# Aggregating a relational graph network with the gathered rows as matmul weights

## The chip, the cores and the metric

The kernel runs on one core of one Trainium2 chip. Its engines are TensorE (PE, with the weight loads shown apart as PEld), VectorE (DVE), ScalarE (ACT), GpSimd (POOL) and SyncE (SP), which share SBUF and run apart, held together by semaphores. The metric is the device time of one launch in microseconds, the median of several runs.

## The reference, cut to what matters

The program is two graph layers, then an attention with random features, then a second attention with low-rank experts. Only the graph layers are touched. There are N = 1250 nodes of D = 768 features, R = 8 relations and 41250 edges, sorted by their destination. One layer is

```
seg  = dst * 8 + etype
sums = segment_sum(x[src], seg);  cnt = segment_sum(1, seg)
mean = (sums / max(cnt, 1)).reshape(N, 8, 768)
out  = einsum('nri,rio->no', mean, W) + x @ root + b
```

Layer 1 is followed by a ReLU, layer 2 takes the result as its x, with its own weights. The 33 edges that a node has on average end in one sum, so that the work can be done as: multiply every node by each of the 8 relation matrices (the messages), fetch for every edge the message of its source and relation, weigh it with 1/cnt, and add it to the row of its destination.

## The kernel before, in words

**Messages.** For each layer and each of 8 relations, PE multiplies 10 blocks of 125 nodes (`RT` = 10, `ROWS` = 125) by a 768x768 panel, in split fp16 (three products of high and low parts, 36 matmuls of 384 columns to a block, `row_products`). ACT and DVE split each result into a high and a low fp16 part (`message_high`, `message`), and SP stores them in DRAM in `msg_table`, one row of 3072 bytes for each node and relation. DVE and ACT meanwhile prepare the next panel (`next_panel`: maximum at t = 0, scales at t = 4, split at t = 6). In layer 1 DVE also counts edges; in the third panel (p = 2, after t = 8) it finds for each group of edges the first and the last block of 125 nodes (`block_extents`), and PE waits for that (`bounds_made`) before the fourth panel.

**Aggregation.** The edges lie in 324 tiles of 128 (`TILES`). POOL fetches each tile with one indirect DMA (L629) into one of `GSLOTS` = 18 slots: 6 in `GATA`, 4 in `ROW`, 2 in `MSG`, and 6 in `WST`, the buffer of the weight panels, so that these last 6 wait for the panel's split (`w_lo`). Tiles are taken in groups of `AT` = 3, 108 groups in 18 turns of 6. For each group PE and DVE loop over the blocks of 125 nodes that it touches; one such step is a pass. There are 117 passes in a layer. In a pass DVE makes for each tile a matrix `HOT` of 128 edges by 125 nodes, which holds the edge's weight where its destination is the node, in a high and a low part (L1280). PE takes `HOT` as weights and moves the gathered rows (L1747): 3 products x 2 halves x 3 tiles = 18 matmuls of 384 columns. The sums lie in PSUM with a node in each partition; DVE adds them to `ROOT`, 125x768 (L1262, `take_pass`), three passes late (`LAG_PASS` = 3). A small matmul of zeros ahead of each group (L1736) tells POOL by the semaphore `group_read` that earlier slots may be filled again: POOL's group g waits for the start of group g - 5.

**The root panel.** x @ root takes 10 more blocks of 36 matmuls. The first 5 run before the passes, the others between turns (`ROOT_AT`). DVE adds each to `ROOT` (L1239), which ACT had set to the bias.

**Between the layers.** DVE takes the maximum of `ROOT` (L1169), from which a scale is made. For each of the 10 blocks ACT writes the ReLU into `ROW`, PE transposes it (6 transposes, L1558) into two PSUM banks, and ACT and DVE split it into the high and low parts of `HT`, feature by node (L732, L1187). The products of the block follow. DVE's order is: `h_low(t)`, the message of block t - 1, `next_panel` for t - 1.

**After layer 2.** The semaphore `rows_done` tells PE to begin the next stage (L1780) and SP to load its next weights and to store `ROOT` in DRAM (`gnn_rows`). Then SP loads `WPR` and three vectors.

The call of the pass loop, where PE waits:

```
pe.wait_ge(S["pass_out"], n + (LAG_PASS * L + 2))
for k in range(AT):
    pe.wait_ge(S["hot_made"], n * AT + (k + 1))
    pe.wait_ge(S[f"gat_in{slot}"], i * 16 + (16 * TURNS * L + 16))
    for hp, mp in ((0, 0), (0, 1), (1, 0)):
        for h in range(2):
```

## Time and profile before

| what | value |
|---|---|
| median of 3 runs | 3300.21 us (3297.36 to 3302.02) |
| span of the profiled execution | 3506.0 us; no other time of this execution is shown |
| mean granted TensorE clock | 0.960 of full speed |
| PE busy | 3182.0 us, 91% |
| DVE busy | 1850.6 us, 53% |
| POOL busy | 1290.4 us, 37% |
| ACT busy | 783.8 us, 22% |
| chain that ended last, by line | L1612 (products of blocks) 25%, L1747 (passes) 20%, L1963 5% |

The span reaches from the first to the last instruction of one execution under the profiler. It is 205.8 us longer than the median of the runs. "Idle before, releaser" says what ended the idle time of an engine: "issue" is that nothing which the profile shows was waited for, and "remote" that the releaser is another core or a queue it does not know. Stages of the span: products of layer 1 to about 597 us, aggregation of layer 1 to 1141 us, products of layer 2 to about 1650 us, aggregation of layer 2 to 2191 us, the two attentions to 3506 us.

### The profile page before, as it was taken

What the parts mean: (1) busy time and instruction counts of PE and PEld (TensorE: products, weight loads), DVE (VectorE), ACT (ScalarE), POOL (GpSimd) and SP (SyncE); (2) the same over time, 40 slices, a digit from 0 to 9 for tenths busy, and PEclk for the clock granted to TensorE, in tenths of its full rate; (3) what the DMA queues carried; (4) which work ended last, traced back from release to release, by engine and by line L of the source; (5) the groups of instructions that cost most, each with busy time, mean ns of one, the idle gap of its engine ahead of it and who ended that gap; (6) DMA issues with size and microseconds to landing.
All of it is one profiled execution on the core that took longest, in us unless ns stands there. A gap on an engine that the chain in (4) does not pass through costs nothing.

```text
span 3506.0 us, 63388 instructions
## 1 busy us (share of the span) xinstructions
PE 3182.0 (91%) x19507; PEld 2353.7 (67%) x19508; DVE 1850.6 (53%) x3025; ACT 783.8 (22%) x1113; POOL 1290.4 (37%) x1388
## 2 busy tenths in 40 slices
PE   6999999888888799999888888999987799999999
PEld 5788888666666688888666666677665555555555
DVE  6576666655555433333555555333458755566551
ACT  1211212000000312122000000444521354544550
POOL 2681112566555000001566655100042156434662
PEclk9999999999999999999999999999999899999999
DMA  4334344677776232324677776300033000000003
GB/s 146 107 121 129 116 143 147 202 246 253 236 241 224 79 110 94 117 93 141 213 247 257 244 242 208 125 13 27 13 89 93 19 19 19 1 19 19 19 25 95
DMA packets 101107, 433.91 MB, mean 124 GB/s; under 512 B 19582, under 2 KB 19920, under 8 KB 96757
## 3 DMA queue, kind: packets, MB, share of 16 engines
q0 software_dynamic: 55712, 266.87, 23.6%
q1 hardware_dynamic: 42533, 124.83, 11.3%
q10 hardware_dynamic: 2736, 40.50, 3.3%
q8 instruction: 83, 1.36, 0.2%
q14 instruction: 43, 0.35, 0.0%
HBM read 355.21 MB, written 76.88 MB: 123 GB/s over the span
## 4 chain that ended last, share of the span: by engine, by line
PE 75%; DVE 11%; issue 8%; DVEq 3%; ACT 2%; POOL 1%; DMA 1%; another core or an unknown queue 0%; POOLq 0%; ACTq 0%; SPq 0%
PE PS L1612 25%; PE PS L1747 20%; PE PS L1963 5%; PE PS L1780 3%; PE PS L1621 3%; PE PS L1893 2%; PE PS L1788 2%; DVE NMC L1534 2%; PE PS L1950 2%; PE PS L1825 2%; PE PS L1809 1%; PE PS L1951 1%; PE PS L1799 1%; PE PS L1817 1%; POOL PL L683 1%
## 5 line engine op out<-in xcount | busy, mean ns | idle before, releaser
L1612 PE MATMUL PS<-WHL,XT 128*125 (+1 forms) x3240 | 557.1, 331 | 15.5 <-issue 6.5
L1612 PE MATMUL PS<-WHL,HT 128*125 (+1 forms) x3240 | 535.5, 327 | 3.7 <-issue 2.5
L1612 PEld LDWEIGHTS PS<-WHL,XT 128*125 128x125 f16 (+1 forms) x3240 | 443.9, 139 | 106.0 <-issue 16.1
L1612 PEld LDWEIGHTS PS<-WHL,HT 128*125 (+1 forms) x3240 | 442.9, 137 | 90.3 <-issue 3.8
L1262 DVE SCALAR_TENSOR_TENSOR ROOT<-PS,GS,ROOT x240 | 244.3, 1018 | 339.7 <-remote 136.9
L683 POOL TENSOR_TENSOR PL<-PF 125x500 bf16<-125x500 f32 (+1 forms) x360 | 322.6, 930 | 216.8 <-ACT PF L897 216.0
L1280 DVE SCALAR_TENSOR_TENSOR HOT<-NODE,DSTF,WHLO (+1 forms) x702 | 298.8, 476 | 129.4 <-issue 120.2
L1123 DVE SCALAR_TENSOR_TENSOR MSG<-PS,MSG 125x768 f16<-125x768 f32 x160 | 153.0, 956 | 361.0 <-ACT MSG L722 359.5
L1747 PE MATMUL PS<-GATA,HOT 128*125 128x384 f16 x1440 | 278.9, 353 | 49.6 <-issue 45.1
L722 ACT ACTIVATE MSG<-PS 125x768 f16<-125x768 f32 x160 | 129.7, 811 | 775.4 <-PE PS L1612 770.3
L1747 PE MATMUL PS<-WST,HOT 128*125 128x384 f16 x1404 | 265.4, 346 | 41.4 <-issue 39.2
L1747 PEld LDWEIGHTS PS<-GATA,HOT 128*125 x1440 | 205.8, 148 | 108.1 <-issue 64.0
L629 POOL DMA_INDIRECT WST<-msg_table,SKEY x216 | 212.3, 983 | 154.5 <-issue 59.3
L629 POOL DMA_INDIRECT GATA<-msg_table,SKEY x216 | 211.4, 979 | 143.7 <-issue 59.7
L1747 PEld LDWEIGHTS PS<-WST,HOT 128*125 x1404 | 197.2, 145 | 96.5 <-issue 56.1
L1963 PE MATMUL PS<-PF,V 125*128 125x500 bf16 (+1 forms) x720 | 244.7, 352 | 16.0 <-POOL PL L683 14.5
L897 ACT ACTIVATE PF<-PS,QK 125x500 f32<-125x500 f32 (+1 forms) x360 | 213.7, 609 | 124.0 <-PE PS L1951 117.8
L1307 DVE RECIPROCAL RCPF<-PS 64x500 f32<-64x500 f32 (+1 forms) x36 | 99.5, 2764 | 198.6 <-PE PS L1963 198.6
L1747 PE MATMUL PS<-ROW,HOT 128*125 128x384 f16 x912 | 174.9, 347 | 23.1 <-issue 21.9
L561 POOL TENSOR_SCALAR LOWHOT<-IOTA,LOF 128x160 bf16<-128x160 bf16 x162 | 151.8, 954 | 96.2 <-DVEq L980 52.0
L1534 DVE TENSOR_REDUCE NMC<-PS 125x2 f32<-125x1000 f32 (+1 forms) x180 | 173.4, 1021 | 18.0 <-PE PS L1931 16.2
L570 POOL TENSOR_SCALAR TMPF<-ETF,GW 128x324 f32<-128x324 f32 x14 | 19.2, 1374 | 420.9 <-DVE GW L1119 417.3
(293 smaller groups left out, 4433.9 us busy)
## 6 DMA issues: line engine op xcount, KB each, us to landing
msg_table<-MSG SPq DMA_DIRECT2D x160, 336.0 KB
WST<-in_wg_dram ACTq DMA_DIRECT2D x16, 2304.0 KB, 10.0
WST<-in_wf_dram SPq DMA_DIRECT2D x7, 1536.0 KB, 6.7
KROW<-key_rows POOLq DMA_DIRECT2D x54, 192.0 KB, 3.8
msg_table<-MSG SPq DMA_DIRECT2D x160, 39.0 KB
WST<-in_wm_dram SPq DMA_DIRECT2D x5, 1152.0 KB, 5.1
GATA<-msg_table,SKEY POOLq DMA_INDIRECT x216
WST<-msg_table,SKEY POOLq DMA_INDIRECT x216
```

The source lines that it names most:

```text
L561: ins = g.tensor_scalar(LOWHOT[:, e % RING, k, :], IOTA[:], LOF[:, e * GRP + k:e * GRP + k + 1], None, ALU.is_equal)
L629: g.indirect_dma_start(out=gat_slot(k), out_offset=None, in_=msg_table, in_offset=bass.IndirectOffsetOnAxis(ap=SKEY[:, t:t + 1], axis=0)). ...
L683: g.tensor_tensor(PL[:, n_ % PARTED, 0:n], PF[:, n_ % PARTED, 0:n], PH[:, n_ % PARTED, 0:n, 1], ALU.subtract).then_inc(S["ffn_lo"], 1)
L722: act.activation(halves(MSG[0:ROWS, t % 2, 0:D]), rowps(2 * (t % 2)), ACT.Copy, scale=MSG_DOWN[L]).then_inc(S["msg_hi"], 1)
L897: act.activation(PF[:, n_ % PARTED, 0:n], p, ACT.Exp, scale=QK[0:ROWS, SSCALE]).then_inc(S["ffn_act"], 1)
L1123: v.scalar_tensor_tensor(halves(MSG[0:ROWS, t % 2, D:2 * D]), rowps(2 * (t % 2)), MSG_DOWN[L], halves(MSG[0:ROWS, t % 2, 0:D]), ALU.mult, ...
L1262: v.scalar_tensor_tensor(rows, pass_psum(n), GS[0:ROWS, 2:3], rows, ALU.mult, ALU.add).then_inc(S["pass_out"], 1)
L1280: v.scalar_tensor_tensor(hot, node, DSTF[:, bass.ds(t, 1)], weight, ALU.is_equal, ALU.mult).then_inc(S["hot_made"], 1)
L1534: v.tensor_reduce(NMC[:, :, s_, c], PS[0:ROWS, ffn.bank(r):ffn.bank(r) + 2, 0:CHUNKS[c][1]], AX.X, ALU.max).then_inc(S["ffn_dve"], 1)
L1612: ins = pe.matmul(PS[0:ROWS, b0 + h, 0:HALF], X[:, xp, k, bass.ts(t, ROWS)], panel_part(slot, wp, k, h), start=k == 0 and xp + wp == 0, st ...
L1747: ins = pe.matmul(PS[0:ROWS, bass.ds((n % LAG_PASS) * 2 + h, 1), 0:HALF].rearrange("p a c -> p (a c)"), HOT[:, bass.ds((n % HOTS) * AT + k ...
L1963: ins = pe.matmul(o, V2[:, vp, t, h, :], parts[pp], start=t == 0 and vp + pp == 0, stop=t == RT - 1 and vp == 1)
```

## The change

The roles in the pass are exchanged. The gathered rows are the weights (128 edges by 128 features), and what moves is the `HOT` of 32 nodes with its high and low part beside each other, 64 columns, and for the low part of the rows the high half alone, 32 columns. The sums lie feature by node: one PSUM bank of [128, 6 x 2 x 32]. Groups have 4 tiles (81 groups), and the nodes of a group are windows of 32 that begin at the group's own first node, so that a group has as many passes as windows of 32 hold its nodes (for 512 sorted edges at 33 to a node, one pass). The groups are written out one after the other, with a loop over the passes in each. The ring has 12 slots, none of them in `WST`. POOL's group g waits for the end of group g - 3, told by a matmul of zeros behind it.

The root panel, the bias and the accumulator `ACC` lie feature by node too: 18 pieces of 128 features by 500 or 250 nodes, 6 before the passes, the others behind every second group. Layer 2's input is split straight from `ACC`, without transposes. Layer 2's result is transposed at the end: 10 blocks of 6 transposes, with a copy by ACT into one of 4 slots of `ROW`, from which SP stores it; PE waits for the last copy (`gnn_made`), and SP issues its loads of `WPR` and of the vectors ahead of these stores. The bounds of the groups are found in another way: a count over 39 thresholds in place of two comparisons.

```diff
-AT = 3
+AT = 4
 AG = TILES // AT
-GSETS = 6
-LAG_PASS = 3
-HOTS = 4
+GSETS = 3
+GSLOTS = GSETS * AT
+WIN = 32
+WINDOWS = -(-N // WIN)
+COLS = N + WIN
+ROOT_FIRST = 6
+PIECES = [(m, c) for c in range(len(CHUNKS)) for m in range(KT)]
+ROOT_BANK = (6, 3)
...
             sp.dma_start(WST[:, 0:WM], a["wm"][128:256, :]).then_inc(S["w_in"], 16)
-            for b in range(RT):
-                move_rows(sp, gnn_rows[b * ROWS:(b + 1) * ROWS, :], ROOT[:, b, :], S["gnn_out"])
-            sp.wait_ge(S["group_used"], 2 * (AG + 1))
             sp.dma_start(WPR[:], a["wmp"]).then_inc(S["wp_in"], 16)
+            sp.wait_ge(S["group_read"], 2 * AG)
             for n_, key in enumerate(("bmp", "gamma", "beta")):
                 sp.dma_start(VEC[:, n_, :], a[key].broadcast_to([ROWS, D])).then_inc(S["vec_in"], 16)
+            for t in range(RT):
+                sp.wait_ge(S["gnn_made"], t + 1)
+                move_rows(sp, gnn_rows[t * ROWS:(t + 1) * ROWS, :], ROW[:, t % 4, :], S[f"gnn_out{t % 4}"])
...
                 for t in range(TILES):
                     grp, k = t // AT, t % GSLOTS
-                    if t == STAGED:
-                        if L == 0:
-                            edge_weights(0)
-                        g.wait_ge(S["w_lo"], (REL + 1) * (L + 1) + 1)
+                    if t == GSLOTS and L == 0:
+                        edge_weights(0)
+                    if t % AT == 0 and L * AG + grp >= GSETS:
+                        g.wait_ge(S["group_read"], L * AG + grp - GSETS + 1)
...
             def h_high(t):
-                act.wait_ge(S["h_t"], t + 1)
-                act.activation(xtview(HT, 0, t), tview(4), ACT.Copy, scale=HSC[:, HSCALE]).then_inc(S["h_hi"], 1)
+
+                act.activation(HT[:, 0, :, t * ROWS:(t + 1) * ROWS], ACC[:, :, t * ROWS:(t + 1) * ROWS], ACT.Relu, scale=HSC[:, HSCALE]).then_inc(S["h_hi"], 1)
...
+            for t in range(RT):
+                act.wait_ge(S["gnn_t"], t + 1)
+                if t >= 4:
+                    act.wait_ge(S[f"gnn_out{t % 4}"], ROW_IN * (t // 4))
+                act.activation(halves(ROW[:, t % 4, :]), rowps(4 + 2 * (t % 2)), ACT.Copy).then_inc(S["gnn_made"], 1)
...
+                v.tensor_scalar(GB[:, 2:3], GB[:, 1:2], 0.0, None, ALU.is_ge)
+                for m in range(1, WINDOWS):
+                    v.drain()
+                    v.scalar_tensor_tensor(GB[:, 2:3], GB[:, 1:2], float(m * WIN), GB[:, 2:3], ALU.is_ge, ALU.add)
...
                 def h_low(t):
 
+                    v.tensor_scalar(HTMP[:], ACC[:, :, t * ROWS:(t + 1) * ROWS], 0.0, HSC[:, HSCALE], ALU.max, ALU.mult)
+                    v.drain()
                     v.wait_ge(S["h_hi"], t + 1)
-                    v.scalar_tensor_tensor(xtview(HT, 1, t), tview(4), HSC[:, HSCALE], xtview(HT, 0, t), ALU.mult, ALU.subtract).then_inc(S["h_free"], 1)
+                    v.tensor_tensor(HT[:, 1, :, t * ROWS:(t + 1) * ROWS], HTMP[:], HT[:, 0, :, t * ROWS:(t + 1) * ROWS], ALU.subtract).then_inc(S["h_free"], 1)
...
+                def make_hots(grp, p):
+
+                    tiles = slice(grp * AT, (grp + 1) * AT)
+                    v.tensor_tensor(SAME[:], NODE[:, bass.ds(p * WIN, WIN)].unsqueeze(1).broadcast_to([128, AT, WIN]),
+                                    DREL[:, tiles].unsqueeze(2).broadcast_to([128, AT, WIN]), ALU.is_equal)
                     v.drain()
+                    v.tensor_tensor(HOT[:, grp % GSETS], SAME[:].unsqueeze(2).broadcast_to([128, AT, 2, WIN]),
+                                    WHLO[:, tiles, :].unsqueeze(3).broadcast_to([128, AT, 2, WIN]), ALU.mult).then_inc(S["hot_made"], 1)
+
+                def take_pass():
...
+                    columns = ACC[:, :, bass.ds(w0, WIN)]
+                    sums = PS[:, bass.ds(bank, 1), 0:KT * 2 * WIN].rearrange("p a (k w c) -> p (a k) w c", w=2, c=WIN)
+                    for w in range(2):
+                        ins = v.scalar_tensor_tensor(columns, sums[:, :, w, :], GS[:, 2:3], columns, ALU.mult, ALU.add)
...
+                for grp in range(AG):
+                    first = v.value_load(LIM[0:1, grp:grp + 1], min_val=0, max_val=N - 1)
+                    n_passes = v.value_load(PASSES[0:1, grp:grp + 1], min_val=1, max_val=WINDOWS)
+                    v.reg_mov(ready, 1)
+                    with v.Fori(0, n_passes) as p:
+                        v.wait_ge(S["pass_done"], v.snap(ready, min_val=1, max_val=1 << 20))
+                        make_hots(grp, p)
+                        take_pass()
...
+                    if grp % 2 == 0 and grp and r < len(PIECES):
+                        take_root(r)
+                        r += 1
...
+                for grp in range(AG):
+                    n_passes = pe.value_load(PASSES[0:1, grp:grp + 1], min_val=1, max_val=WINDOWS)
+                    pe.reg_mov(taken, 1)
+                    with pe.Fori(0, n_passes):
+                        pe.wait_ge(S["pass_out"], pe.snap(taken, min_val=1, max_val=1 << 20))
+                        pe.wait_ge(S["hot_made"], pe.snap(cnt, min_val=0, max_val=1 << 20) + 1)
+                        for k in range(AT):
+                            t = grp * AT + k
+                            pe.wait_ge(S[f"gat_in{t % GSLOTS}"], 16 * (TILES // GSLOTS * L + t // GSLOTS + 1))
+                            rows = gat_slot(t % GSLOTS)
+                            for c in range(KT):
+                                o = PS[:, grp % GSETS, c * 2 * WIN:(c + 1) * 2 * WIN]
+                                pe.matmul(o, rows[:, c * 128:(c + 1) * 128], HOT[:, grp % GSETS, k].rearrange("p w c -> p (w c)"), start=k + c == 0, stop=False)
+                                ins = pe.matmul(o[:, 0:WIN], rows[:, D + c * 128:D + (c + 1) * 128], HOT[:, grp % GSETS, k, 0, :], start=False, stop=k == AT - 1 and c == KT - 1)
+                        ins.then_inc(S["pass_done"], 1)
...
+                    pe.matmul(PS[:, 7, 320:322], ZERO[:, 0:128], ZERO[:, 0:2], start=True, stop=True).then_inc(S["group_read"], 1)
+                    if grp % 2 and r < len(PIECES):
+                        root_piece(r)
+                        r += 1
 
             pe.wait_ge(S["rows_done"], 2)
+            for t in range(RT):
+                if t >= 2:
+                    pe.wait_ge(S["gnn_made"], t - 1)
+                for k in range(KT):
+                    ins = pe.transpose(PS[0:ROWS, 4 + 2 * (t % 2) + k // 3, (k % 3) * 128:(k % 3 + 1) * 128], ACC[:, k, t * ROWS:(t + 1) * ROWS], IDF[:])
+                ins.then_inc(S["gnn_t"], 1)
+            pe.wait_ge(S["gnn_made"], RT)
```

## Rows read from the trace of the kernel before

**Rows 1.** The page: its head, and a group of weight loads (columns: busy us, mean ns of one, idle before).
```profile
span 3506.0 us, 63388 instructions
...
L1612 PEld LDWEIGHTS PS<-WHL,XT 128*125 128x125 f16 (+1 forms) x3240 | 443.9, 139 | 106.0 <-issue 16.1
```

**Rows 2.** Busy time by stage: length, busy of PE, PEld, DVE, ACT, POOL, clock, DMA.
```profile
630.00:1141.00 511.00, 425.80 (x2358) 331.35 (x2358) 274.86 (x475) 0.00 (x0) 308.61 (x312) 0.92 0.74 241
...
1680.00:2191.00 511.00, 430.17 (x2384) 335.91 (x2382) 276.01 (x475) 0.00 (x0) 304.56 (x312) 0.92 0.74 241
```

**Rows 3.** Groups of POOL's instructions, 630 to 1141 us (a fourth, MSG x34, left out).
```profile
L629 POOL DMA_INDIRECT WST<-msg_table,SKEY x108 | 106.6, 987 | 75.5 <-issue 29.8 <-PE PS L1736 21.4 <-remote 17.6
L629 POOL DMA_INDIRECT GATA<-msg_table,SKEY x102 | 100.2, 982 | 70.5 <-PE PS L1736 31.0 <-issue 26.9 <-remote 12.6
L629 POOL DMA_INDIRECT ROW<-msg_table,SKEY x68 | 67.6, 994 | 38.6 <-issue 16.8 <-PE PS L1736 16.7 <-remote 5.1
```

**Rows 4.** Groups of DVE's instructions in the same stretch.
```profile
L1280 DVE SCALAR_TENSOR_TENSOR HOT<-NODE,DSTF,WHLO (+1 forms) x350 | 148.7, 476 | 59.1 <-issue 54.4
L1262 DVE SCALAR_TENSOR_TENSOR ROOT<-PS,GS,ROOT x120 | 122.1, 1018 | 176.2 <-remote 73.2 <-PE PS L1747 68.0 <-issue 35.1
```

**Rows 5.** The timeline of PE: start, us, what.
```profile
722.52 3.09 PE L1747 MATMUL PS<-GATA,HOT 128*125 128x384 f16 x18
...
725.50 3.09 PE L1747 MATMUL PS<-ROW,HOT 128*125 128x384 f16 x18
```

**Rows 6.** The timeline of all engines, with the idle time before each.
```profile
638.93 1.02 POOL L629 DMA_INDIRECT GATA<-msg_table,SKEY  x1 [0.68 <-issue]
...
657.55 1.02 DVE L1262 SCALAR_TENSOR_TENSOR ROOT<-PS,GS,ROOT  x1 [2.48 <-remote]
...
657.62 4.81 PE L1747 MATMUL PS<-GATA,HOT 128*125 128x384 f16 x18 [1.74 <-issue]
658.07 0.96 POOL L629 DMA_INDIRECT WST<-msg_table,SKEY  x1 [2.56 <-remote]
```

**Rows 7.** The timeline of POOL at the end of layer 1.
```profile
1126.41 1.22 POOL L629 DMA_INDIRECT WST<-msg_table,SKEY  x1 [0.31 <-issue]
```

**Rows 8.** Busy time by stretches of 10 us; the last columns are clock, DMA share, GB/s.
```profile
600.00:610.00 10.00, 9.75 (x55) 7.64 (x54) 3.25 (x15) 0.00 (x0) 5.73 (x6) 0.85 0.89 303
...
1130.00:1140.00 10.00, 9.37 (x57) 7.56 (x57) 4.54 (x7) 0.00 (x0) 0.00 (x0) 1.00 0.02 10
```

**Rows 9.** The chain that ended last: start, us, what.
```profile
578.70 5.85 PE PS L1612 x36
...
1217.18 35.10 PE PS L1612 x216
...
2213.96 10.42 PE PS L1788 x180
...
2259.75 19.03 PE PS L1780 x108
```

**Rows 10.** The timeline between the layers.
```profile
1141.48 8.15 DVE L1169 TENSOR_REDUCE HMX<-ROOT 125x1 f32<-125x7680 f32 x1
...
1156.36 7.53 PE L1612 MATMUL PS<-WHL,HT 128*125 128x384 f16 x36
```

**Rows 11.** The timeline of DVE at two places.
```profile
262.00 0.96 DVE L1123 SCALAR_TENSOR_TENSOR MSG<-PS,MSG 125x768 f16<-125x768 f32 x1 [2.06 <-ACT MSG L722]
...
589.25 0.16 DVE L1131 RECIPROCAL GS<-GS 128x1 f32<-128x1 f32 x1
589.49 0.15 DVE L1133 TENSOR_SCALAR GS<-GS 128x1 f32<-128x1 f32 x1
```

**Rows 12.** The timeline at the end of layer 2's passes.
```profile
2189.76 1.02 DVE L1262 SCALAR_TENSOR_TENSOR ROOT<-PS,GS,ROOT  x1 [1.95 <-PE PS L1747]
...
2193.07 20.88 PE L1780 MATMUL PS<-XT,WHM 128*128 128x500 f16 x108 [3.65 <-issue]
```

**Rows 13.** A DMA issue from 2190 to 2260 us: KB, us to landing.
```profile
WPR<-in_wmp_dram SPq DMA_DIRECT2D x1, 2304.0 KB, 10.6
```

More of the change, by code:

```diff
@@ L61 @@
 PARTED = 6
-ROW_SUMS = (REL + 1) * RT
+ROW_SUMS = REL * RT
 SHIFT = 2.0 ** 15
@@ L1243, in root_row @@
+                for r in range(ROOT_FIRST):
+                    if L == 0 and r < TAIL:
+                        take_counts(REL, r, r == TAIL - 1)
+                        if r == TAIL - 1:
                             inverse_weights()
-                    if t == 0:
+                    take_root(r)
+                    if r == 0:
                         panel_max(nq, ncols)
-                    elif t == 2:
+                    elif r == 2:
                         top_row(nq)
-                    elif t == 3:
+                    elif r == 3:
@@ L1298, in _ @@
+                take_pass()
                 v.drain()
@@ L1686, in _ @@
                     pe.wait_ge(S["bounds_made"], 1)
-                    for n_ in range(2):
-                        ins = pe.transpose(PS[0:1, 5, n_ * AG:(n_ + 1) * AG], GB[:, 2 + n_:3 + n_], IDF[0:AG, 0:AG])
-                    ins.then_inc(S["bounds_t"], 1)
+                    pe.matmul(PS[:, 5, 0:2 * AG], ONEK[:], DIAG[:].rearrange("p a g -> p (a g)"), start=True, stop=True).then_inc(S["bounds_t"], 1)
                 else:
-                    transpose_h(0)
                     pe.wait_ge(S["w_lo"], REL + 2)
@@ L1711, in weights_top, with root_piece @@
                         top_broadcast((REL + 1) * (L + 1))
-                for t in range(ROOT_AT[L][0][1]):
-                    row(REL, t, t % 2)
-                    if L == 0 and t < TAIL:
-                        find_counts(REL * RT + t - COUNTED * RT)
-                    weights_top(t)
+                def root_piece(r):
+                    m, c = PIECES[r]
+                    c0, n = CHUNKS[c]
+                    if len(PIECES) * L + r >= 2:
+                        pe.wait_ge(S["root_out"], len(PIECES) * L + r - 1)
+                    for k in range(KT):
+                        for wp, xp in ((0, 0), (0, 1), (1, 0)):
+                            ins = pe.matmul(PS[:, ROOT_BANK[r % 2], 0:n], WHL[:, (REL + L) % 2, wp, k * D + m * 128:k * D + (m + 1) * 128], X[:, xp, k, c0:c0 + n],
+                                            start=k == 0 and wp + xp == 0, stop=k == KT - 1 and wp == 1)
+                    ins.then_inc(S["root_done"], 1)
@@ L1754, in _ @@
-                for n_, (i, t) in enumerate(ROOT_AT[L]):
-                    root_row(t)
-                    if n_ == 0:
-                        q0 = pe.snap(cnt, min_val=0, max_val=1 << 20)
-                        for z in range(LAG_PASS):
-                            for h in range(2):
-                                ins = pe.matmul(PS[0:ROWS, bass.ds(((q0 + z) % LAG_PASS) * 2 + h, 1), 0:HALF].rearrange("p a c -> p (a c)"), ZERO[:, 0:ROWS], ZERO[:], start=True, stop=True)
-                            ins.then_inc(S["pass_done"], 1)
-                    passes(i, ROOT_AT[L][n_ + 1][0] if n_ + 1 < len(ROOT_AT[L]) else TURNS)
```

245 lines of the change are left out of this document (92 added, 153 removed).

## The prediction

> **What bounds the kernel now.** I read the busy time by stage first. The change touches two stages in full, the aggregations, and both are 511 us long in the trace [rows 2]. Neither has an engine that works throughout: PE 426 to 430 us, POOL 305 to 309 us, DVE 275 us, the DMA engines 74%. So waits set the length, and I looked for whose.
>
> POOL comes next. In the first stage it issues 312 gathers (12 came earlier). One takes 0.99 us [rows 2, 3], and behind each lies 0.3 us of issue (29.8 + 26.9 + 16.8 us over some 250), so a gather costs POOL 1.28 us, and 312 cost 399 us whatever else happens. The rest of 511 us is waiting: in the three groups shown 69 us end with L1736, PE's signal of a free slot, and 35 us with "remote" [rows 3]; and 14 us pass from the last gather's end at 1127.6 us [rows 7] to the stage's end at 1141.5 us [rows 10]. In that tail the DMA engines are already at 2% from 1130 us on [rows 8]: the data is there, PE has some groups left.
>
> PE's own work is close behind: a pass takes 2.98 us (722.52 to 725.50) [rows 5], 117 passes 349 us, and five root blocks of 5.85 us [rows 9] 29 us: 378 us. DVE has 3 x 0.476 + 1.018 = 2.4 us in a pass [rows 4], 287 us. So POOL at 399 us and PE at 378 us plus its loop turns are nearly equal, and each makes the other wait now and then.
>
> Last, the odd waits. At 657.6 us PE begins a group whose first gather was issued at 638.9 us; DVE and POOL start again within half a microsecond of it, after 2.5 us of "remote" [rows 6]. The three wait for nothing of each other there. I take this for the profiler. The span is 3506.0 us [rows 1], 205.8 us over the median of 3300.21 us, and that excess must lie somewhere: in the products PE is too busy to hold it (5.85 us for 36 matmuls [rows 9] is the same in block after block), so most lies in the aggregations. If all of it does, a stage is 511 - 103 = 408 us without the profiler; if only POOL's "remote" time is the profiler's, it is 476 us. I take 425 us, nearer to the first because the excess has no other place of that size. The sum is made against the span, and the same difference is carried to the median.
>
> **The change, part by part.**
>
> *The passes.* A pass has 4 tiles x 6 x 2 = 48 pairs of a weight load and a short matmul; 81 passes. No row has matmuls of 64 or 32 columns. Upper neighbour: L1788, with 125 columns of weights loaded for each matmul of 128 columns, 10.42 us for 180, 58 ns [rows 9]. Lower bound: 64 and 32 columns at the rate of 384 in 162 ns, mean 20 ns. I take 55 ns, since the load stays when the matmul shrinks: 2.6 us, 214 us in all (78 to 226 us). The far upper bound is a load fully exposed, 139 ns [rows 1], 6.7 us a pass. The rule that speaks against the change is the Trainium skill's, page "TensorE: Matmul & The Clock Gate", section "LDWEIGHTS (loading the stationary operand)": a load takes its columns / 1.2 ns, 107 ns for 128. By it a pass is 5.1 us and PE would be the bound (a rival below); by the row's 58 ns it is 2.8 us. The row disagrees, for it holds load and matmul in 58 ns.
>
> *The root panel.* Layer by layer 18 pieces of 18 matmuls, which are three times the 108 matmuls of L1780 (500, 500 and 250 columns), 19.03 us [rows 9]: 57.1 us against ten blocks, 58.5 us. 12 pieces, 34 us, lie among the passes. PE: 214 + 34 = 248 us, with a microsecond a group for waits and loops 330 us. That is below POOL's 399 us.
>
> *DVE.* For each group two operations on 128 and 256 elements for the one-hots (0.476 us for 250 [rows 4]; I take 0.7 us together) and two of 192 from PSUM (1.018 us for 768; 0.7 us together), issue as now (59.1 + 35.1 us over 117 passes [rows 4], 0.8 us), and two register loads that no row prices alone; with 0 to 1.5 us for them 2.2 to 3.7 us, against POOL's 4 x 1.28 = 5.1 us. Hidden by POOL; without that cover it would set 180 to 300 us.
>
> *The ring of 12.* A group's slots must come free 15.4 us after its first gather is issued, before POOL needs them. Issue takes 5.1 us, landing no more than some 3 to 5 us (DMA traffic ends within 3 us of the last gather [rows 7, 8]), PE handles each tile as it lands, 0.7 us for the last, and a root piece ahead of it adds up to 3.8 us. That is 15 us at the very worst, so POOL should seldom wait. POOL's new wait is queued before its own gathers alone. The DMA engines then carry 128 x 3072 bytes per 1.28 us, 307 GB/s; they have carried 303 GB/s at 89% [rows 8].
>
> So a stage becomes 399 us of POOL and a tail of 6 us (landing 3, the last tile 0.7, two DVE operations, semaphores), 405 us: 20 us less than 425, from 3 us (408) to 71 us (476). Two stages: -40 us.
>
> *Start of the stages.* Gathers 13 to 18 no longer wait for `WST`, but the 13th now waits for PE's first group. Six pieces are 22.8 us of PE where five blocks were 29 us, and DVE's split comes as much earlier at most. I take -2 us for each layer, -4 us (-12 to +8).
>
> *Between the layers.* The eight blocks from 1156.36 to 1217.18 us [rows 9, 10] take 7.6 us each in place of 5.85: transposes and their two banks. They go. What stays is DVE's long maximum and its split, each of which holds `h_low` up by some 3.2 us: -14 + 6.4 = -7.6 us. The first block loses its transposes and the copy before them, -2.4 us. Together -10 us (-16 to -3).
>
> *Bounds of groups.* 39 dependent tiny operations of DVE. Such operations follow each other in 0.24 us (589.25 to 589.49) [rows 11], 9.4 us. They stand between two messages of the third panel, ahead of the message at 262.00 us [rows 11], and PE waits for both; the slack is about the 2.06 us of that row, less the new reductions. +8 us (+2 to +11).
>
> *After layer 2.* Now PE starts L1780 2.3 us after DVE's last operation (2189.76 + 1.02 to 2193.07) [rows 12]. In the new kernel ten blocks are transposed, copied by ACT in about 1 us each and stored. From the fifth on ACT waits for the store of the block four before. These stores stand on SP's queue behind 1152 + 2304 + 3 x 375 KB of loads; `WPR` alone took 10.6 us to land [rows 13]. At some 330 GB/s the loads take 14 us, the first store lands at 16 us, copies 5 to 8 follow at the pace of the stores until 20 us, the last two until 22 us, and PE waits for the last. Lower bound, if the stores don't queue: ten copies, +9 us; upper, if each store waits its turn and PE starts slow, +30 us. I take +18 us.
>
> **The sum.** -40 - 4 - 10 + 8 + 18 = -28 us: span 3478 us, median 3300 - 28 = 3272 us. The forecast's own range is 3245 to 3300 us.
>
> **Rivals.**
>
> 1. *POOL's gather is dearer in the trace than in a run.* If 1.1 us were its price without the profiler, PE's 378 us and turns bound the kernel before (408 us), and the new one takes 343 + 6 = 349 us: -118 us for the stages, 3300 - 118 + 12 = 3194 us. The case in which the stage was 476 us gives 3170 us. For it: PE and POOL are close. Against: 0.95 and 0.3 us repeat without spread. 0.20.
> 2. *The gain is small and the side costs eat it.* Stages 408 us before, 405 us after: -6 - 4 - 10 + 8 + 18 = +6 us, 3306 us; 3290 to 3312 us with the bounds near. 0.14.
> 3. *The weight loads make PE the bound.* This is the case of the Trainium skill's rule above. It decides from where 48 pairs, 0.42 us of root work and 0.3 us of the group's own pass 5.1 us, that is from 91 ns a pair. At 100 ns a group is 5.5 us and a stage 446 + 6 us, 27 us over 425: 3300 + 54 + 12 = 3366 us. At 139 ns 7.4 us a group, 605 us, 3672 us. For it: nothing here has matmuls shorter than their loads, and a PE that works half of the time may be granted 1.2 GHz in place of 2.4. Against: 58 ns [rows 9], and a PE that falls behind is busy throughout, which is when rows show full clock. 0.10.
> 4. *The group's own steps show.* Register loads on DVE and PE, and code that is no longer reused, in each of 81 groups; if a slot returns so late that a group takes 1 us more than POOL's 5.1 us, a stage is 486 us, 3300 + 122 + 12 = 3434 us; half of that 3352 us. For it: DVE's "issue" idle time [rows 4]. Against: the slack of the ring. 0.07.
>
> The forecast has 0.49. About 0.2% is what a measurement of this kernel can tell from no change, 3293.6 to 3306.8 us. Faster: 0.43 of the forecast, rival 1, 0.03 of rival 2: 0.66. Same: 0.05 and 0.06: 0.11. Slower: 0.23. The range of 8 in 10 runs from rival 1 with its upper part, 3175 us, to the nearer part of rivals 3 and 4, 3345 us.
>
> **What the new profile would show.** L1747's successor with some 7800 pairs at 45 to 60 ns in bursts; POOL's gathers at 1.28 us with hardly an idle time ended by PE; the stage's tail at 6 us; blocks of layer 2's first panel at 5.9 us but for two; a gap of PE of some 9 us near 260 us; some 20 us of PE's waiting for ACT's copies after layer 2. Wrong would be: POOL waiting for PE in most groups (3 or 4), POOL's pitch below 1.28 us in the runs' time (1), or copies that never wait for stores.

## The result and the profile after

The changed kernel takes 3314.23 us (median of 6 runs, 3310.68 to 3317.14) against 3301.11 us (6 runs of the kernel before beside them): ratio 1.0041, 95% interval 1.0029 to 1.0053. It is slower by 0.4%, 13 us, where the prediction had it faster by 28. A second comparison gave 1.0037 (1.0024 to 1.0050). The profiled execution took 3310.68 us, with a span of 3308.9 us.

The page of the changed kernel, its head and slices (busy share and granted clock of TensorE in tenths):

```profile
span 3308.9 us, 66031 instructions
...
PE   6998999765555999999755558999986999999999
...
PEclk9999999885555999999865559999997999999999
```

TensorE is half idle in both aggregations and its clock falls to 0.5, the lower of its two levels (1.2 of 2.4 GHz). So the change did lighten its work. The stages by stretch, as [rows 2] showed them before:

```profile
640.00:1034.00 394.00, 226.15 (x4087) 180.49 (x4087) 130.70 (x330) 0.00 (x0) 298.91 (x312) 0.61 0.91 311
1570.00:1963.00 393.00, 229.51 (x4074) 182.49 (x4075) 130.48 (x329) 0.00 (x0) 297.18 (x311) 0.60 0.91 311
```

The groups of GpSimd and TensorE between the 13th and the last gather of layer 1, which answer to [rows 3] (busy us, mean ns; idle before and its releasers):

```profile
L618 POOL DMA_INDIRECT GATA<-msg_table,SKEY x156 | 149.9, 961 | 60.0 <-issue 46.0 <-PE PS L1744 14.0
L618 POOL DMA_INDIRECT ROW<-msg_table,SKEY x104 | 99.6, 958 | 32.0 <-issue 30.8 <-PE PS L1744 1.2
L618 POOL DMA_INDIRECT MSG<-msg_table,SKEY x52 | 50.7, 974 | 15.8 <-issue 14.9 <-PE PS L1744 0.9
...
L1739 PE MATMUL PS<-HOT,GATA 128*128 128x64 f16 x948 | 87.7, 209 | 86.3 <-DMA GATA<-msg_table,SKEY 74.3 <-DVE HOT L1262 10.1 <-DVE ACC L1274 1.3
L1740 PE MATMUL PS<-HOT,GATA 128*128 128x32 f16 x948 | 85.8, 203 | 0.0
```

GpSimd issues a gather every 0.96 + 0.30 us and waits almost never for TensorE: 16 us in all, 12.7 of them ahead of the 13th gather, where the window opens. TensorE waits for gathered rows. That is as forecast. What was wrong can't be seen here: it is the kernel before.

### The profile page after: what moved, and what is told of

It reads as the page before. It is cut to its first block, busy times and chain, and to the rows that moved or that the text cites. A ratio compares the mean times of both kernels' runs of the same rounds, so it can differ in the third digit from the quotient of the medians.

```text
span 3308.9 us, 66031 instructions
## 1 busy us (share of the span) xinstructions
PE 2769.4 (84%) x22935; PEld 2024.6 (61%) x22935; DVE 1577.5 (48%) x2801; ACT 783.9 (24%) x1105; POOL 1277.4 (39%) x1388
## 3 DMA queue, kind: packets, MB, share of 16 engines
q1 hardware_dynamic: 42417, 124.07, 11.8%
## 4 chain that ended last, share of the span: by engine, by line
PE 56%; POOL 15%; DVE 11%; issue 10%; DMA 3%; DVEq 2%; ACT 2%; SPq 0%; POOLq 0%; ACTq 0%
PE PS L1614 24%; POOL GATA L618 7%; PE PS L1955 5%; POOL ROW L618 4%; PE PS L1772 3%; PE PS L1623 3%; PE PS L1885 3%; POOL MSG L618 2%; PE PS L1780 2%; DVE NMC L1535 2%; PE PS L1942 2%; PE PS L1817 2%; PE PS L1801 2%; PE PS L1943 2%; PE PS L1791 2%
## 5 line engine op out<-in xcount | busy, mean ns | idle before, releaser
L1614 PE MATMUL PS<-WHL,XT 128*125 (+1 forms) x2880 | 487.5, 329 | 7.0 <-DVE WHL L1030 4.2
L1614 PEld LDWEIGHTS PS<-WHL,XT 128*125 (+1 forms) x2880 | 391.0, 138 | 83.0 <-issue 4.6
L618 POOL DMA_INDIRECT GATA<-msg_table,SKEY x324 | 310.3, 958 | 116.0 <-issue 95.2
L1739 PE MATMUL PS<-HOT,GATA 128*128 128x64 f16 x1944 | 180.2, 209 | 184.3 <-DMA GATA<-msg_table,SKEY 153.0
L1739 PEld LDWEIGHTS PS<-HOT,GATA 128*128 128x128 f16 x1944 | 149.9, 118 | 211.1 <-DMA GATA<-msg_table,SKEY 97.7
L1274 DVE SCALAR_TENSOR_TENSOR ACC<-PS,GS,ACC x328 | 137.2, 418 | 232.1 <-PE PS L1740 183.9
L618 POOL DMA_INDIRECT ROW<-msg_table,SKEY x216 | 206.6, 957 | 67.1 <-issue 64.0
L1739 PE MATMUL PS<-HOT,ROW 128*128 128x64 f16 x1296 | 124.0, 211 | 113.9 <-DMA ROW<-msg_table,SKEY 104.6
L1739 PEld LDWEIGHTS PS<-HOT,ROW 128*128 128x128 f16 x1296 | 101.6, 119 | 133.3 <-DMA ROW<-msg_table,SKEY 81.2
L1740 PE MATMUL PS<-HOT,GATA 128*128 128x32 f16 x1944 | 176.2, 203 | 0.0
## 6 DMA issues: line engine op xcount, KB each, us to landing
WST<-in_wg_dram ACTq DMA_DIRECT2D x16, 2304.0 KB, 10.1
```

Of the source, the lines that this page charges most:

```text
L618: g.indirect_dma_start(out=gat_slot(k), out_offset=None, in_=msg_table, in_offset=bass.IndirectOffsetOnAxis(ap=SKEY[:, t:t + 1], axis=0)). ...
L1274: ins = v.scalar_tensor_tensor(columns, sums[:, :, w, :], GS[:, 2:3], columns, ALU.mult, ALU.add)
L1614: ins = pe.matmul(PS[0:ROWS, b0 + h, 0:HALF], X[:, xp, k, bass.ts(t, ROWS)], panel_part(slot, wp, k, h), start=k == 0 and xp + wp == 0, st ...
L1739: pe.matmul(o, rows[:, c * 128:(c + 1) * 128], HOT[:, grp % GSETS, k].rearrange("p w c -> p (w c)"), start=k + c == 0, stop=False)
L1740: ins = pe.matmul(o[:, 0:WIN], rows[:, D + c * 128:D + (c + 1) * 128], HOT[:, grp % GSETS, k, 0, :], start=False, stop=k == AT - 1 and c = ...
```

## The experiments

Each ratio below is against the kernel before, run beside it. The gains of single edits over the changed kernel go by its two ratios, 1.0041 and 1.0037.

**The kernel before, profiled again.** No edit.

> The kernel before, unchanged, profiled again. The prediction took its two aggregation stages as 425 us each. Theory now: a run without the pauses of the first profile has its stages at GpSimd's pitch, 324 gathers x 1.256 us = 407 us from first to last gather, the span is close to 3299 us, and the other parts of the kernel stay where the first profile had them. So the change had 5 us a stage to win, not 20. Rival: the stages take 425 us or more here too, with waits for ring slots between the gathers, and then some other part of the kernel was shorter than the first profile showed.

Measured: ratio 0.9997 (0.9987 to 1.0007). The head of its page and its two stages:

```profile
span 3295.8 us, 63388 instructions
...
626.00:1028.00 402.00, 382.05 (x2328) 309.81 (x2329) 271.53 (x473) 0.00 (x0) 305.35 (x312) 0.99 0.89 303
1571.00:1972.00 401.00, 382.88 (x2351) 311.05 (x2350) 271.40 (x473) 0.00 (x0) 304.12 (x311) 1.00 0.89 304
```

The groups of GpSimd in the first of them, once more the rows of [rows 3]:

```profile
L629 POOL DMA_INDIRECT WST<-msg_table,SKEY x108 | 106.1, 983 | 39.4 <-issue 30.5 <-DVE WHL L941 6.7 <-PE PS L1736 2.1
L629 POOL DMA_INDIRECT GATA<-msg_table,SKEY x102 | 99.9, 980 | 32.5 <-issue 29.9 <-PE PS L1736 2.7
```

"Remote" is gone, and the waits for TensorE went from 31.0 and 21.4 us to 2.7 and 2.1. The 511 us of [rows 2] are 409.2 here (626.4 us, the 13th gather, to 1035.6 us, the operation that follows the last sum). So the theory holds: GpSimd already set the stage before the change, with TensorE at 95% just beneath it (the next run tests that). The second stage, counted alike, is 408.9 us in place of 510.8, so the two aggregations held 204 of the first profile's surplus of 210 us. With a profile that has no such pauses the whole difference can be laid out. The marks are starts of instructions in the two timelines:

| stretch | before, again | after | difference | predicted |
|---|---|---|---|---|
| start to first gather | 590.9 | 600.5 | +9.6 | +8 (bounds) |
| to the 13th gather | 35.5 | 38.8 | +3.3 | -2 |
| to the last gather | 401.6 | 394.4 | -7.2 | -20, with the tail |
| to the maximum of the hidden rows | 7.6 | 7.6 | 0 | |
| to layer 2's first product | 14.9 | 12.4 | -2.5 | -2.4 |
| to layer 2's first gather | 494.6 | 496.4 | +1.8 | -7.6 |
| to its 13th | 26.4 | 20.3 | -6.1 | -2 |
| to its last | 400.7 | 393.0 | -7.7 | -20, with the tail |
| to the mixer's first product | 10.1 | 35.5 | +25.4 | +18 |
| to the end | 1313.6 | 1310.0 | -3.6 | 0 |
| sum | 3295.8 | 3308.9 | +13.1 | -28 |

The rows are rounded one by one. A mark can move by some us from profile to profile: the first gather of the changed kernel is at 600.5 us here and at 604.3 us in its second profile below.

**Is TensorE's relief worth anything? A third of its products left out of the kernel before.**

```diff
-for hp, mp in ((0, 0), (0, 1), (1, 0)):
+for hp, mp in ((0, 0), (1, 0)):
```

> The kernel before, without the product of the one-hots' high part with the rows' low part: a third of the aggregation's products left out (some 160 us of TensorE's 490 us of them). Theory: TensorE was busy 95% of the stage but GpSimd's gathers set its pace (324 at 0.98 + 0.30 us), so each stage stays at 395 to 402 us and the time falls by less than 10 us. Rival: TensorE was the bound and GpSimd only kept up with it: then both stages get shorter, until another engine stops them, and the time falls by 15 us or more.

Measured: 3298.76 us against 3298.53, ratio 0.9999 (0.9990 to 1.0009). The window of the first stage:

```profile
626.00:1025.00 399.00, 302.21 (x1635) 213.44 (x1633) 274.05 (x474) 0.00 (x0) 301.49 (x308) 0.98 0.89 302
```

TensorE has 302 us of work in place of 382 and the stage, 13th to last gather, is 399.3 us in place of 401.6. The kernel before had nothing to gain from less TensorE work in this place: TensorE's load fell by a fifth (382 to 302 us) and the stage by 2 us.

**Bytes or gathers? Half rows in the changed kernel.**

```diff
-g.indirect_dma_start(out=gat_slot(k), out_offset=None, in_=msg_table,
+g.indirect_dma_start(out=gat_slot(k)[:, 0:D], out_offset=None, in_=msg_table.rearrange("r (w c) -> (r w) c", w=2),
```

> The changed kernel, each gather fetching 128 half rows of 768 elements (1.5 KB) instead of 3 KB, so that half of the bytes are left out; TensorE uses the high parts in place of the low ones, with as many products as before. Theory: GpSimd issues one gather every 1.26 us whatever it carries (0.96 us of work and 0.30 us between), and that sets the stage; the two stages stay at 394 us from the thirteenth gather to the last, and the time stays within 5 us. Rival: the transfers set the pace (the 16 DMA engines were 91% busy at 311 GB/s): each stage falls towards 200 us and the time by 200 us or more.

Measured: ratio 1.0032 (1.0022 to 1.0042), as the changed kernel's own 1.0041 and 1.0037. The window, and then the first group of GpSimd over 640 to 1034 us:

```profile
640.00:1030.00 390.00, 222.52 (x4062) 179.89 (x4059) 130.15 (x328) 0.00 (x0) 294.83 (x308) 0.60 0.56 156
```

```profile
L618 POOL DMA_INDIRECT GATA<-msg_table,SKEY x156 | 149.6, 959 | 60.0 <-issue 45.7 <-PE PS L1744 14.3
```

The DMA engines fall from 91% to 56% and from 311 to 156 GB/s, and the gathers keep their pitch. A DMA share of 91% was no bound.

**Fewer gathers in the changed kernel.**

```diff
+                    if t % AT == AT - 1:
+                        continue
                     g.indirect_dma_start(out=gat_slot(k), out_offset=None, in_=msg_table,
...
-                            t = grp * AT + k
+                            t = grp * AT + min(k, AT - 2)
```

> The changed kernel without the gather of every fourth tile (a quarter of the edges left out; TensorE uses the third tile's rows a second time, with as many products as before). Theory: 243 gathers instead of 324 at 1.26 us take 304 us if only their number counts, so each stage falls by about 100 us (80 to 102) and the time by 160 to 200 us. Rival: TensorE's own work (0.95 us a tile at the clock granted there, 230 us in all, and its waits for the one-hots and for the sums) keeps the stage above 350 us: then the time falls by less than 90 us.

Measured: 3143.39 us, ratio 0.9522 (0.9508 to 0.9537), 171 us less than the changed kernel. The theory holds in size: from the 13th to the last gather the stages take 302.9 and 302.6 us in place of 394.4 and 393.0. But TensorE no longer waits for rows:

```profile
L1741 PE MATMUL PS<-HOT,GATA 128*128 128x64 f16 x905 | 73.4, 209 | 74.3 <-DVE HOT L1264 74.3
...
L620 POOL DMA_INDIRECT GATA<-msg_table,SKEY x128 | 122.7, 959 | 45.7 <-issue 37.6 <-PE PS L1746 8.1
```

TensorE waits for VectorE's one-hots in place of the DMA. VectorE is the next bound, close below, and the next run shows how close.

**Groups of three tiles: that part of the change undone.**

```diff
-AT = 4
+AT = 3
-GSETS = 3
+GSETS = 4
+SUM_BANK = (0, 1, 2, 5)
```

(and `grp % GSETS` becomes `SUM_BANK[grp % GSETS]` where a bank of sums is named).

> The changed kernel with groups of 3 tiles and four banks of sums (12 slots, as before) in place of groups of 4 and three banks: this part of the change undone alone. 108 groups instead of 81, so a third more one-hot pairs (0.29 + 0.42 us) and additions (2 x 0.42 us) on VectorE, from 131 to about 175 us of the stage's 394. Theory: GpSimd's 1.26 us a gather still sets the stage and the time stays within 5 us of the changed kernel's. Rival: a group's own steps (its register loads, the zero product, the waits around it) show: at 0.5 us or more a group, 27 more groups in two stages cost 25 us or more. Second rival: smaller groups come free sooner, so the stalls of GpSimd for slots (16 us in the first stage) go, and the time falls by 10 us.

Measured: 3332.78 us, ratio 1.0105 (1.0090 to 1.0119), 18 us above the changed kernel beside it (3314.74 us; 22 us by the two ratios). The theory, that GpSimd alone sets the pace, fails here, and the first rival holds, a little under its 25 us. TensorE's groups over the stage and VectorE's timeline of one group:

```profile
L1740 PE MATMUL PS<-HOT,GATA 128*128 128x64 f16 x947 | 80.0, 212 | 102.6 <-DVE HOT L1263 102.6
```

```profile
802.01 0.26 DVE L1260 TENSOR_TENSOR SAME<-NODE,DREL 128x96 f16<-128x96 f16 x1 [1.66 <-issue]
802.34 0.43 DVE L1263 TENSOR_TENSOR HOT<-SAME,WHLO 128x192 f16<-128x192 f16 x1
803.12 0.42 DVE L1275 SCALAR_TENSOR_TENSOR ACC<-PS,GS,ACC  x1 [0.34 <-issue]
803.71 0.42 DVE L1275 SCALAR_TENSOR_TENSOR ACC<-PS,GS,ACC  x1 [0.17 <-issue]
806.19 0.26 DVE L1260 TENSOR_TENSOR SAME<-NODE,DREL 128x96 f16<-128x96 f16 x1 [2.06 <-issue]
```

A group costs VectorE 3.7 to 4.2 us (802.01 to 806.19, and 806.19 to 809.91 for the next), of which 1.5 us is work and 1.7 to 2.1 us is "issue" ahead of the first operation, where its two register loads and the loop's turn stand (what part each has isn't shown). Three gathers cost GpSimd 3 x 1.26 = 3.8 us: the two are level. That each hitch of VectorE's is then a loss that is never made up is a reading, not shown by a run. The 324 gathers of the two layers last 3 and 6 us longer, and what follows the last gather 4.2 and 5.5 us (11.8 us to the maximum in place of 7.6, 41.0 us to the mixer in place of 35.5). With four tiles a group has 5.0 us for some 3.5 us of VectorE's (4.57 us from the group at 803.79 us of the changed kernel to the next, of which 1.09 us is a wait for TensorE). In the run with three gathers of four, 81 groups of some 3.8 us are 308 us, as long as its 243 gathers.

**The bounds of groups in two operations.**

```diff
-                v.tensor_scalar(GB[:, 2:3], GB[:, 1:2], 0.0, None, ALU.is_ge)
-                for m in range(1, WINDOWS):
-                    v.drain()
-                    v.scalar_tensor_tensor(GB[:, 2:3], GB[:, 1:2], float(m * WIN), GB[:, 2:3], ALU.is_ge, ALU.add)
+                v.tensor_scalar(DIAG[:, 0, 0:WINDOWS], CST[0:AG, 0:WINDOWS], float(WIN), GB[:, 1:2], ALU.mult, ALU.is_le)
+                v.drain()
+                v.tensor_reduce(GB[:, 2:3], DIAG[:, 0, 0:WINDOWS], AX.X, ALU.add)
```

> The changed kernel, with the chain of 39 dependent VectorE steps that counts a group's windows replaced by one comparison of 40 limits and one sum. Theory: the chain took 9.0 us of the profile and TensorE waited 8.2 us for it (and for nothing else), so the time falls by 8 us (7 to 9), to 3306. Rival: TensorE and VectorE catch up with that wait before the first gather, because the panels that follow wait for weights anyway: less than 3 us.

Measured: ratio 1.0010 (1.0001 to 1.0019): 9 to 10 us less. The timelines, first of the changed kernel, then of this one:

```profile
259.13 9.03 DVE L1055 SCALAR_TENSOR_TENSOR GB<-GB 81x1 f32<-81x1 f32 x39
268.24 0.43 DVE L1058 TENSOR_SCALAR DIAG<-IDF,GB 81x81 f32<-81x81 f32 x2
...
268.75 0.64 PE L1683 MATMUL PS<-DIAG,ONEK 81*128 81x162 f32 x1 [8.19 <-DVEq L1059]
```

```profile
258.92 0.27 DVE L1052 TENSOR_SCALAR DIAG<-CST,GB 81x40 f32<-81x40 f32 x1
259.26 0.19 DVE L1054 TENSOR_REDUCE GB<-DIAG 81x1 f32<-81x40 f32 x1
```

The first gather moved from 600.5 us to 591.2 us, so the 9 us of the chain were on the path to it in full. The three profiles with this edit have it at 589.9 to 591.9 us, the seven others of the changed kernel and its variants at 599.8 to 604.3 us.

**The hidden rows split one tile further ahead** (on ScalarE and on VectorE alike).

```diff
-                    for t in range(RT + 1):
-                        if t < RT:
-                            h_low(t)
+                    h_low(0)
+                    for t in range(RT + 1):
+                        if t + 1 < RT:
+                            h_low(t + 1)
```

> The changed kernel, with the splitting of the hidden rows one tile further ahead on ScalarE and VectorE (the halves of tile t+1 are made before the messages of tile t-1 instead of behind them). Theory: TensorE's four waits for VectorE's half of a tile (2.7, 1.9, 2.4 and 2.5 us in the first relation of layer 2) took the place of the transposes that the change removed; with the halves ready ahead they go, and the time falls by 9 us (6 to 10), to 3305. Rival: VectorE and ScalarE are themselves the bound there (4.9 us for a panel's maximum, 5.0 us for its low part), so that the waits only move to the messages' buffers: less than 3 us.

Measured: ratio 1.0006 (0.9997 to 1.0015), 10 to 12 us less. TensorE's timeline in layer 2's first relation, changed kernel and then this one:

```profile
1053.71 14.07 PE L1614 MATMUL PS<-WHL,HT 128*125 128x384 f16 x72 [2.57 <-issue]
1070.45 13.59 PE L1614 MATMUL PS<-WHL,HT 128*125 128x384 f16 x72 [2.67 <-DVE HT L1183]
...
1086.06 11.91 PE L1614 MATMUL PS<-WHL,HT 128*125 128x384 f16 x72 [1.91 <-DVE HT L1183]
```

```profile
1054.38 25.97 PE L1616 MATMUL PS<-WHL,HT 128*125 128x384 f16 x144 [2.57 <-issue]
...
1080.29 11.86 PE L1616 MATMUL PS<-WHL,HT 128*125 128x384 f16 x72
```

The four waits are gone. From the first product of layer 2 to its first gather 483.1 us pass in place of 496.4. That is 13.3 us for 9.5 us of waits. Part of the rest goes with the clock: the third and fourth block take 13.6 us in the changed kernel and 11.9 us here, and the stretch of 12 us in which the first wait falls (from 1065.7 us) was granted 0.86, the same stretch here 1.00. The other 2 us were not traced.

**The stores ahead of the loads.** SyncE's ten pairs of stores are moved, as a block, from behind the loads of `WST`, `WPR` and `VEC` to ahead of them.

```diff
+            for t in range(RT):
+                sp.wait_ge(S["gnn_made"], t + 1)
+                move_rows(sp, gnn_rows[t * ROWS:(t + 1) * ROWS, :], ROW[:, t % 4, :], S[f"gnn_out{t % 4}"])
             sp.dma_start(WST[:, 0:WM], a["wm"][128:256, :]).then_inc(S["w_in"], 16)
             sp.dma_start(WPR[:], a["wmp"]).then_inc(S["wp_in"], 16)
...
-            for t in range(RT):
-                sp.wait_ge(S["gnn_made"], t + 1)
-                move_rows(sp, gnn_rows[t * ROWS:(t + 1) * ROWS, :], ROW[:, t % 4, :], S[f"gnn_out{t % 4}"])
```

> The changed kernel, with SyncE's ten pairs of stores of the second layer's rows issued ahead of the loads of the second mixer panel, of the mixer's output weights and of the three vectors. Theory: behind those loads (about 4 MB) a store of 384 KB takes 12 us, and the last six copies wait for a buffer that it holds; alone it takes 3 to 4 us, so the time falls by 8 us (6 to 11), to 3306. The stretch from the end of the sums to the mixer's first product falls from 29 to about 20 us. Rival: the transposes and copies themselves, ten at 1.4 to 2 us, set that stretch: no change within 2 us. Second rival: the second mixer panel now comes so late that the second mixer turn waits for it, and the gain is given back.

Measured: ratio 1.0001 (0.9992 to 1.0010), 12 to 13 us less. ScalarE's copies in the changed kernel:

```profile
1976.12 0.81 ACT L792 ACTIVATE ROW<-PS 125x768 f32<-125x768 f32 x1 [0.47 <-PE PS L1754]
1991.36 1.72 ACT L792 ACTIVATE ROW<-PS 125x768 f32<-125x768 f32 x2 [14.42 <-DMA gnn_rows<-ROW]
```

And in this one:

```profile
1981.09 0.81 ACT L792 ACTIVATE ROW<-PS 125x768 f32<-125x768 f32 x1 [0.35 <-DMA gnn_rows<-ROW]
```

One wait of 14.42 us for a buffer becomes waits of less than 0.7 us; last gather to mixer falls from 35.5 to 22.2 us. That is more than the 8 us expected (6 to 11): from the last sum to the mixer 28 us became 14, not 20. The second rival doesn't hold: TensorE waits for no load of weights in the first 150 us of the mixer. What follows the mixer's first product is 1316.4 us in this profile and 1310.0 us in the changed kernel's, but the run with the short bounds, which leaves this place alone, has 1316.2 us too, so that difference isn't put down to the edit.

**The three edits together.**

> The changed kernel with the three edits together: stores ahead of the loads, bounds by one comparison and one sum, and hidden rows split one tile further ahead. Each alone gained 14.7, 11.1 and 11.6 us against the changed kernel's 3314.2, with about 3 us of noise in each. Theory: they lie in three different places of the chain that ends last (bounds at 258 us, first relation of layer 2 at 1054 us, the join at 1964 us) and add up: 31 us less (24 to 37), 3283 us, 0.5% faster than the kernel before. Rival: part of each gain was one and the same change of the program (its code or its buffers lie differently): then the sum is 15 to 20 us, 3296 us, and no difference from the kernel before can be measured.

Measured: 3278.34 us, ratio 0.9935 (0.9921 to 0.9949), 0.65% faster than the kernel before and 34 to 36 us faster than the changed one. The gains add up. In its profile the stretches are 591.9 us to the first gather, 483.1 us from layer 2's first product to its first gather, 21.6 us from the last gather to the mixer, and 393.4 and 393.0 us between the 13th and the last gather: the stages are what they were. No run gave the kernel before the edits that it could have too (the halves ahead above all), so how much of the 0.65% belongs to the exchange of roles isn't shown.

**What the layout costs at the end: no turn at all.** The same kernel without the 60 transposes and 10 copies; the stored rows hold something else.

> The changed kernel with the three edits together, and in addition without turning the second layer's sums back into rows: the 60 transposes and 10 copies between the last sums and the mixer are left out, and SyncE stores rows with other contents. This prices what the layout by features costs at the end. Theory: 22 us lie between the last gather and the mixer's first product with the turn and 10 us in the kernel before, so the time falls by 12 us (9 to 14) against the three edits together, to 3266. Rival: something else holds the mixer's start (its panel, buffers), then it falls by less than 5 us.

Measured: ratio 0.9904 (0.9890 to 0.9919), 10 us below the three edits. Last gather to mixer is 10.2 us, as in the kernel before (10.1).

**The changed kernel again.**

> The changed kernel as it is, beside the kernels of this call and on the same chip. It should come out 11 to 17 us above the kernel before again (ratio 1.003 to 1.005), as in its first comparison; its profile's marks (first gather near 600, last gather to mixer 35 us) should repeat within 3 us. Rival: the 0.4% was the scatter between two loads of a program; then the ratio is within 0.1% of 1, and the three single edits of the earlier call gained less than was read from them.

Measured: 3314.74 us, ratio 1.0037 (1.0024 to 1.0050). First gather at 604.3 us, 3.8 us later than in the first profile and so outside the 3 us expected; last gather to mixer 37.2 us.

## Why the prediction was wrong

**The step that failed** is "I take 425 us" for a stage of the kernel before. The text had the right value in its hands: if all of the excess of 205.8 us over the median lay in the aggregations, a stage was 408 us. A profile without that excess shows 409.2 us, and the other bound, 476 us, rested on the label "remote" alone. A value between the two was no estimate: one followed from a sum that had to close, the other from a label. So the two stages had -6 us to give by the text's own 405 us, and not -40. They gave -14.9 us. In the first stage that is 7.2 us: a gather costs GpSimd 0.981 us before and 0.962 us after (312 x 0.019 = 6.0 us), its waits for TensorE between the 13th and the last gather went from 6.9 to 3.4 us, and its "issue" gaps grew by 2.3 us. Why the gather itself became cheaper isn't shown; less TensorE work alone did not do it (0.979 us in the run with a third of the products left out).

Forecast and result are 41 us apart: 25 us lie in the stages, 9 us between the layers, 7 us after layer 2, 3 us in the bounds and the starts of the stages, and 4 us of the other sign in what follows (each rounded).

This is rival 2, "the gain is small and the side costs eat it", 3306 us with 3290 to 3312, given 0.14. It came out at 3314, and the terms say where the other 8 us are.

**Between the layers**, -10 us predicted, -0.7 us found. The prediction took the eight blocks' 7.6 us apiece [rows 9, 10] as 5.85 us of products and 1.75 us of transposes and banks, which would go. But of the 1.75 us the transposes were 0.65 us, as the second profile of the kernel before shows by their starts and the products'. Most of the rest was TensorE's waits for VectorE's half of a tile, one in every second block. TensorE's transposes in the kernel before (1050 to 1120 us), then its products in the changed one (1053 to 1120 us):

```profile
L1558 PE MATMUL PS<-IDF,ROW 125*128 125x125 f32 x52 | 7.6, 283 | 6.0 <-DVE HT L1187 6.0
```

```profile
L1614 PE MATMUL PS<-WHL,HT 128*125 128x384 f16 x308 | 56.6, 350 | 12.0 <-DVE HT L1183 9.4 <-issue 2.6
```

So four waits of 1.3 to 1.8 us, 6.0 us in all, were there before the change and are 9.5 us after it (1.9 to 2.7 us each). With 8 x 0.65 = 5.2 us of transposes gone, 3.5 us of waits more, and the third and fourth block at 13.6 us in place of 12.0, the eight blocks take 61.3 us either way.

Where the waits come from stands in VectorE's order: half of tile t, message of t - 1, `next_panel` for t - 1. `next_panel` has a part at t = 0, 2, 4 and 6, and each part holds up the next half. Two are the long operations that the prediction counted, the maximum (4.94 us) and the split (5.01 us). The other two it left out: VectorE waits there for a small matmul (L1576, L1581) that comes in TensorE's order behind the two blocks that it is at work on. VectorE's timeline in the changed kernel at the first of them:

```profile
1079.07 0.96 DVE L1117 SCALAR_TENSOR_TENSOR MSG<-PS,MSG 125x768 f16<-125x768 f32 x1 [6.09 <-ACT MSG L711]
1084.19 0.28 DVE L912 TENSOR_REDUCE TOPP<-PS 1x1 f32<-1x128 f32 x1 [4.16 <-PE PS L1576]
1084.40 0.59 DVE L1180 TENSOR_SCALAR HTMP<-ACC,HSC 128x750 f32<-128x750 f32 x1
```

The edit that makes the halves one tile further ahead takes all four waits away, 13.3 us of the stretch. So there was a gain to be had here, but 6.0 us of it lay in an order that the kernel before had too.

**After layer 2**, +18 us predicted, +25.4 us found. The mechanism was right to the instruction: the fifth copy waits for the first store, which is behind the loads. The term was mis-sized: the first store landed at 1991.3 us, some 21 us after the first transposes' start, not 16. SyncE's issue of the first of its two parts took 6.05 us, where those behind it take 0.3 to 1.1 us, and the second part, issued at 1979.2 us, took 12.05 us. SyncE's queue in the timeline, and then the chain that ended last:

```profile
1973.13 6.05 SPq L379 DMA_DIRECT2D gnn_rows<-ROW  x1
1979.22 0.88 SPq L380 DMA_DIRECT2D gnn_rows<-ROW  x1
```

```profile
1970.60 5.50 PE PS L1754 x24
...
1979.22 12.05 DMA gnn_rows<-ROW
```

Of the 25 us, 13 are the order on the queue and 11 the turn itself, by the two experiments.

**Bounds**: +8 predicted, +9.6 found, and 9.3 us came back with the two-operation form. **Start of the stages**: -4 predicted, +3.3 and -6.1 found, -2.8 in sum.

**The passes.** The price of a pair, taken as 55 ns with bounds of 20 and 139 ns, is 27 to 28 ns at the granted clock of 1.0 and 40 ns at 0.5. It was wrong and cost nothing, since GpSimd sets the stage. The neighbour, 58 ns a pair [rows 9], was misread: its own 128 moving columns take 54 ns at the rate of 384 in 162 ns, so it says little of what a load costs. The rule of the Trainium skill (page "TensorE: Matmul & The Clock Gate", section "LDWEIGHTS (loading the stationary operand)") that stood behind rival 3 gives a load of 128 columns 107 ns. The trace shows such a duration for the single load and not for the pitch of many, as the last section shows. The Trainium skill's next section on the same page, "Weight-path perf modes — Fast Weight Load (FWL) and DoubleRow", says that loads of exactly 128 columns of a type other than FP32 are read in four chunks in parallel. The same section of the Trainium skill gives four times the speed in theory for fp8, and about twice as measured on Trainium2. The pitch of 27 ns, a quarter of 107, agrees with it in kind and is more than twofold, and the prediction should have weighed it: the loads of the neighbour have 125 columns. No run here changed the columns of a load alone, so that this is the reason isn't shown; a limit on how fast such short pairs are issued isn't excluded. **Rival 1**, that GpSimd's gather is dearer in the trace than in a run, falls: with the gather at its 1.26 us, the span of the second profile is the time of its run to 2 us (3295.8 and 3297.6), and a third less of TensorE's products moved nothing. **Rival 4**, the group's own steps, did not come true: a group of four costs VectorE some 3.5 us, near the top of the 2.2 to 3.7 us that the text gave, and GpSimd's 5.0 us cover it. But it was near: with groups of three it is 3.7 to 4.2 us against 3.8, and 18 us of time.

**What is left open**: whether the start of the first stage (+3.3 us, one group of four before a slot comes back where three were enough) can be had back, and the 3.6 us by which the mixer and what follows is shorter (1310.0 against 1313.6 us); it is 1311.5 us in the second profile of the changed kernel and up to 1316.4 us in its variants.

## What to carry to other kernels

When a profile's span is 6% over the median of the runs, take the profile again or close the sum first: put the excess where it can lie before costing anything, and don't average it with a label. When a change relieves an engine, ask which engine stands right beneath it: here a stage with TensorE at 95% had GpSimd at the same length, and a third of its products left out moved it by 2 us. When blocks take longer than their products, ask the trace what fills the difference before counting it as the work that the change removes: here it was in the main waits that stayed. And look at every order around the engine that is relieved (who makes its input, how far ahead, and what stands in front of its output on a queue): here an old order, a new one and a chain of small operations cost 34 to 36 us and could be put right in a few lines.

## What the runs showed of the hardware

A weight load and its matmul can follow each other faster than a load's own duration. TensorE's weight loads at 666 us of the changed kernel, where the clock was full:

```profile
666.12 0.10 PEld L1739 LDWEIGHTS PS<-HOT,GATA 128*128 128x128 f16 x1 [1.67 <-DVE HOT L1262]
666.14 0.10 PEld L1740 LDWEIGHTS PS<-HOT,GATA 128*128 128x128 f16 x1
666.17 0.10 PEld L1739 LDWEIGHTS PS<-HOT,GATA 128*128 128x128 f16 x1
```

Each takes 0.10 us and the next starts 0.02 to 0.03 us later, each with a matmul of 64 or 32 columns of its own. At the lower clock (granted 0.50) the matmuls start 0.05 and 0.03 us apart in turn (1962.14, 1962.17, 1962.22, 1962.25 us), in the order of the 64 and 32 columns; at the full clock both take 0.027 us.

A gather of 128 rows costs GpSimd 1.26 us from one to the next, the same for 3 KB and for 1.5 KB a row, and the DMA engines' share of 0.91 was not the sign of a bound: with half of the bytes it was 0.56 at the same pace.

The granted clock of TensorE was 0.50, its lower level, in the aggregations (760 to 800 us, with TensorE busy 20.6 us of 40, after 1.00 in the products ahead of the stage). Nothing of that shows in the length of the stage, where TensorE waits for rows; 0.81 was granted in the first 12 us of the products that came after, and 0.86 in the next 12.
